# Mixture-of-experts stage with tiles of 128 slots in place of 256

## The reference

```python
def _L0_ffn_ref(x, gate_w, expert_bias, w_up, w_down):
    B, S, H, E, K, I = (4, 512, 256, 8, 2, 1024)
    logits = jnp.einsum('bsh,eh->bse', x, gate_w) + expert_bias
    weights = jax.nn.softmax(logits, axis=-1)
    top_w, top_i = jax.lax.top_k(weights, K)
    top_w = top_w / (jnp.sum(top_w, axis=-1, keepdims=True) + GATE_EPS)
    sparse_w = jnp.sum(jax.nn.one_hot(top_i, E, dtype=weights.dtype) * top_w[..., None], axis=-2)
    out = jnp.zeros_like(x)
    for e in range(E):
        h = jax.nn.gelu(jnp.einsum('bsh,ih->bsi', x, w_up[e]), approximate=False)
        y = jnp.einsum('bsi,hi->bsh', h, w_down[e])
        out = out + sparse_w[..., e:e + 1] * y
    mu = jnp.mean(out, axis=-1, keepdims=True)
    var = jnp.mean(jnp.square(out - mu), axis=-1, keepdims=True)
    out = (out - mu) * jax.lax.rsqrt(var + LN_EPS)
    return out + x
x = x + _L0_xattn_ref(_layernorm(x, axis=-1), ctx_1024, ctx_1024, L0_xattn_Wq, ...)
x = x + _L0_ffn_ref(_layernorm(x, axis=-1), L0_ffn_gate_w, ...)
```

## Time and profile before

| what | value |
|---|---|
| median of 3 runs | 841.6 us (840.79 to 843.38) |
| profiled execution, span | 841.2 us |
| TensorE matmuls busy | 738.7 us (88%) |
| VectorE / ScalarE / GpSimd busy | 561.5 / 363.6 / 443.2 us |
| mean granted TensorE clock | 0.932 of full |

### The profile page before, as it was taken

The page is one execution under the profiler, slowest core; times in us unless marked ns, Lnnn a source line. Parts: engine busy times, 40 slices in busy tenths (PEclk is TensorE's granted clock), DMA queues, the critical chain, the costliest instruction groups (busy, mean ns, idle before and its releaser), DMA issues.

```text
span 841.2 us, 20449 instructions
## 1 busy us (share of the span) xinstructions
PE 738.7 (88%) x6144; PEld 665.2 (79%) x6145; DVE 561.5 (67%) x1215; ACT 363.6 (43%) x657; POOL 443.2 (53%) x584
## 2 busy tenths in 40 slices
PE   4999999999999934599999999999999999999300
PEld 4899999999999832288989999999999999898200
DVE  4899898998989758565555555555555555554195
ACT  2777777777777711122222222222222222222185
POOL 3677777777777623534444444444444444432287
PEclk9999999999999965589999999999999999999755
DMA  4233333233232110011111111111111111110494
GB/s 154 94 103 107 114 98 108 99 106 112 96 115 91 51 39 0 25 39 52 52 51 50 50 50 44 44 50 50 45 49 44 50 50 50 50 37 26 144 312 169
DMA packets 39874, 64.52 MB, mean 77 GB/s; under 512 B 5408, under 2 KB 30240, under 8 KB 39840
## 3 DMA queue, kind: packets, MB, share of 16 engines
q1 hardware_dynamic: 31632, 42.37, 15.7%
q0 software_dynamic: 7488, 20.46, 7.6%
q10 hardware_dynamic: 720, 1.26, 0.4%
HBM read 45.46 MB, written 18.61 MB: 76 GB/s over the span
## 4 chain that ended last, share of the span: by engine, by line
PE 87%; DVE 4%; issue 3%; POOL 2%; DMA 1%; ACT 1%; SPq 0%; DVEq 0%; POOLq 0%; ACTq 0%
PE ps_a L527 25%; PE ps_b L541 24%; PE ps_a L387 7%; PE ps_b L430 7%; PE ps_c L409 3%; PE ps_c L414 3%; PE ps_b L397 3%; PE ps_a L465 3%; PE ps_a L452 2%; PE ps_c L495 2%; PE ps_c L511 2%; PE ps_a L476 1%; PE ps_c L377 1%; PE ps_a L440 1%; PE ps_c L422 1%
## 5 line engine op out<-in xcount | busy, mean ns | idle before, releaser
L527 PE MATMUL ps_a<-area,w_hi 128*128 128x256 f16 x1248 | 208.8, 274 | 1.7 <-DVE area L792 1.7
L541 PE MATMUL ps_b<-w_hi,area 128*128 x1248 | 206.4, 273 | 0.0
L1052 POOL DMA_INDIRECT y_rows<-area x78 | 78.0, 1001 | 209.2 <-ACT area L937 197.3
L527 PE MATMUL ps_a<-area,w_lo 128*128 128x256 f16 x624 | 171.1, 274 | 0.0
L541 PE MATMUL ps_b<-w_lo,area 128*128 x624 | 170.1, 273 | 0.0
L932 ACT ACTIVATE area<-ps_a 128x512 f32<-128x512 f32 x156 | 93.2, 598 | 143.1 <-PE ps_a L527 141.7
L527 PEld LDWEIGHTS ps_a<-area,w_hi 128*128 x1248 | 122.8, 98 | 16.4 <-issue 2.1
L541 PEld LDWEIGHTS ps_b<-w_hi,area 128*128 128x128 f16 x1248 | 122.1, 98 | 14.1
L790 DVE TENSOR_SCALAR area<-ps_c 128x512 f16<-128x512 f32 x39 | 27.0, 692 | 151.7 <-PE ps_c L511 151.7
L802 DVE SCALAR_TENSOR_TENSOR area<-area 128x512 f16<-128x512 f32 x156 | 108.3, 694 | 5.4
L1042 POOL DMA_INDIRECT area<-xn_rows,area x78 | 77.7, 996 | 46.9 <-issue 35.9
(11 more groups left out here) (130 smaller groups left out, 1263.8 us busy)
## 6 DMA issues: line engine op xcount, KB each, us to landing
area<-weights SPq DMA_DIRECT2D x32, 512.0 KB, 3.3
w_hi<-y_rows SPq DMA_DIRECT2D x32, 256.0 KB, 4.6
resid<-x_in SPq DMA_DIRECT2D x32, 128.0 KB, 2.1
area<-ctx_t SPq DMA_DIRECT2D x32, 128.0 KB, 2.1
xn_rows<-area SPq DMA_DIRECT2D x32, 128.0 KB, 1.7
out<-w_lo SPq DMA_DIRECT2D x16, 256.0 KB, 2.7
area<-xn_rows,area POOLq DMA_INDIRECT x78
y_rows<-area POOLq DMA_INDIRECT x78
```

The source lines that it names most:

```text
L527: mm = pe.matmul(ps_h[:, q, (ic % 2) * SLOTS:(ic % 2 + 1) * SLOTS], w[:, bass.ds(first + (hc * I + ic * P), P)], r[b][:, hc, :], start=(n ...
L541: mm = pe.matmul(ps_y[:, b, v * D:(v + 1) * D], g[b][:, ic, v * P:(v + 1) * P], w[:, bass.ds(first + (EXPERT_COLS + ic * D), D)], start=(n ...
L1052: pool.indirect_dma_start(y_rows[:, :], bass.IndirectOffsetOnAxis(ap=didx[b][:, v:v + 1], axis=0), y_s[b][:, v * D:(v + 1) * D], None).the ...
```

## The change

SUBS goes from 2 to 1, so a tile has 128 slots and there are 71 tiles. A gather, a scatter, and one of down's two passes over the 24 products fall away from each tile; up keeps its 48 matmuls and 48 weight loads a tile, with 128 moving columns. Four chunks now fill a PSUM bank, so a tile's h takes two banks, GQ is 2, and two tiles of h lie in PSUM and two in g_s. Waits on g_r and gl_r go back two tiles in place of one. The loop covers tiles 4 to 68.

```diff
-SUBS = 2
+SUBS = 1
...
-        GQ = 4
-        g_s = [carve(512) for _ in range(GQ)]
+        GQ = 2
+        g_s = [[carve(512) for _ in range(GQ)] for _ in range(2)]
...
-        MOE_FIRST, MOE_LAST = 4, 36
+        MOE_FIRST, MOE_LAST = 4, 68
...
-                    q = ic // 2
-                    if ic % 2 == 0:
-                        since(pe, g_r, GQ * (k - 1) + q + 1)
+                    q, i = ic // (IC // GQ), ic % (IC // GQ)
+                    if i == 0:
+                        since(pe, g_r, GQ * (k - 2) + q + 1)
                     n = 0
                     for hc in range(HC):
                         for w, r in ((w_hi, xt_hi), (w_hi, xt_lo), (w_lo, xt_hi)):
-                            mm = pe.matmul(ps_h[:, q, (ic % 2) * SLOTS:(ic % 2 + 1) * SLOTS],
+                            mm = pe.matmul(ps_h[:, GQ * b + q, i * SLOTS:(i + 1) * SLOTS],
                                            w[:, bass.ds(first + (hc * I + ic * P), P)], r[b][:, hc, :],
                                            start=(n == 0), stop=(n == 3 * HC - 1))
                             n += 1
-                    if ic % 2:
+                    if i == IC // GQ - 1:
                         mm.then_inc(h_ps, 1)
...
-                    src = ps_x[:, b, :].rearrange("p (c n) -> p c n", c=HC)
+                    src = ps_x[:, b, 0:HC * SLOTS].rearrange("p (c n) -> p c n", c=HC)
...
-                        src = g_s[q].rearrange("p (c n) -> p c n", n=SLOTS)
+                        src = g_s[b][q].rearrange("p (c n) -> p c n", n=SLOTS)
...
-                        since(act, gl_r, GQ * (k - 1) + 1 + q)
-                        act.activation(g_s[q], ps_h[:, q, :], ACT.Gelu, scale=1.0 / (X_SCALE * W_SCALE)).then_inc(g_r, 1)
+                        since(act, gl_r, GQ * (k - 2) + 1 + q)
+                        act.activation(g_s[b][q], ps_h[:, GQ * b + q, :], ACT.Gelu, scale=1.0 / (X_SCALE * W_SCALE)).then_inc(g_r, 1)
...
-                    act.activation(y_s[b], ps_y[:, b, :], ACT.Copy, scale=1.0 / (G_SCALE * W_SCALE)).then_inc(y_r, 1)
+                    act.activation(y_s[b], ps_y[:, b, 0:SUBS * D], ACT.Copy, scale=1.0 / (G_SCALE * W_SCALE)).then_inc(y_r, 1)
```

## The result

The changed kernel takes 979.67 us (median of 4 runs, 978.93 to 979.96) where the kernel before takes 842.01 (median of 4, the three known ahead of the prediction and one more): a ratio of 1.163, 95% interval 1.162 to 1.165. The prediction said 974, range 940 to 1030, slower with 0.94. The profiled execution of the changed kernel took 978.93 us and has a span of 977.1: 1.8 us of a launch lie outside the span, where the text ahead of the prediction has nothing. The prediction's 974 is added up from a span, so it is to be held against 977.1.

A forecast was written before the change was run, and what follows sets the result against it. TensorE's array bounds the expert stage before; after the change its sequencer does, 7.94 us a tile against 5.5 of array. Span 841.2 + 136.8 (stage) - 3.8 (small terms) = 974 us, range 940 to 1030 (its own 950 to 1005).

The forecast's parts named there:

- The bound: Expert stage after the change: TensorE's sequencer needs 7.94 us a tile against 5.5 of array, stage +136.8 us.
- The turn: Expert loop on the sequencer, two tiles: first tile 8.26 us, second 7.61; a loop turn of 15.9 us.
- the groups of three matmuls: Up and down: three matmuls with their register instructions take 0.24 us of sequencer, 16 groups in up, 8 in down.
- The reads: Expert number read ahead of up and down: 0.75 to 0.9 us each, 1.5 with the loop's turn, no longer hidden.
- The small terms: Outside the tile loop: first gather -1.3, last scatter -1.3, routing products -1.3, larger expert table +0.1; together -3.8 us.
- The array as the bound: Rival, expert stage: sequencer keeps ahead, a tile costs 5.5 us, kernel gains, 802 us; chance 0.05.
- Reads that hide: Rival, expert stage: only up's 80 ns pace counts, reads and loop turn hide behind queued matmuls, 885 us; chance 0.05.
- Loads that do not hide: Rival, up: 128-column matmuls stay at 109 ns, 8.1 us of array a tile, 999 us; chance 0.05.
- The falling clock: Rival, expert stage: TensorE idle about a third, clock falls; a third of tiles at low clock, 1040 us; chance 0.07.
- the second set of h banks: PSUM banks and g_s in the expert stage: second set removes waits that before does not show; costed at nothing.
- the gathers two tiles ahead: Expert stage: a tile's gather is issued two tiles ahead, 16 us, where landing took 2.8; costed at nothing.
- the other engines: Expert stage, per tile: VectorE 3.0 us, ScalarE 1.5, GpSimd about 3.5, each under 7.94, so off the path.

The follow-up runs named there:

- the test of the reads alone: Changed kernel without the two reads of slot_expert a tile, weights' place worked out from the tile's number, register instructions kept in the loop: 875.39 us, ratio 1.040.

## Why the prediction was right

**The bound.** It moved where the prediction put it: from the array to TensorE's sequencer. Constant addresses take 178 us away at 128 slots and none at 256, and the loop's turn is the sum of the sequencer's own steps.

**The terms.** The turn was forecast at 15.87 us and is 16.18. Up and down together take 12.0 us of the sequencer in a turn where 11.72 were forecast, so the groups of three matmuls take 0.25 us and not 0.24. The reads were within 0.1 us each. The loop makes 32 turns (64 tiles, 4 to 67). From its entry at 386.8, the second line below, to its last branch at 904.9 they take 518.1 us, 10.3 more than the forecast has for them. The rest of the stage, seven tiles, first matmuls and drain, takes 55.5 us, 4.5 less than the 60.0 left for it; these tiles have no turn, and no further cause of the 4.5 is shown. The stage runs from the transposes at 350.28 to the last matmul's end at 923.62 + 0.27, 573.6 us, where 567.8 was forecast:

```profile
350.28 0.66 PE L511 MATMUL ps_c<-cst,area 128*128 128x128 f32 x2 [5.60 <-DMA area<-xn_rows,area]
...
L290 PEldq MOVE  x1: 29/29/29, 386.8 to 386.8; - x1
...
352.08 0.39 PE L527 MATMUL ps_a<-area,w_hi 128*128 128x128 f16 x2 [1.14 <-DVE area L792]
...
923.62 0.27 PE L541 MATMUL ps_b<-w_lo,area 128*128 x1
```

**The small terms** were forecast at -3.8 and came to -6.7: the stage begins 3.7 us earlier than in the earlier trace rows, and from the last matmul to the end it is 53.2 us in place of 56.2. In the first, the routing matmuls take 16.90 us in place of 18.25 and the first gather leads to the first transposes in 3.0 us (347.25 to 350.28) in place of 4.5; each is close to its forecast of -1.3. Another 0.9 us lie ahead of them, and 0.7 of these arise between 300 and 305 us, at the end of attention, which the change leaves alone. There the same matmuls ran at the low clock in the trace before (first line, granted clock 0.50 from 301.0 to 301.8) and still at 1.00 in the trace after (second line):

```profile
301.01 0.70 PE ps_a L440 x2
...
300.94 0.45 PE ps_a L440 x2
```

That is chance between two executions. In the second part, one scatter less is 1.5 us, and the other 1.5 lie in the combine, which the change leaves alone too. In sum 142.6 - 6.7 = +135.9 us on spans of 841.2 and 977.1.

**What was luck.** The mechanism and the terms were right, but that the sum came within 3 us of the span is partly luck. The loop was forecast 10 us too short; the tiles outside it gave 4.5 us back and the small terms 2.9, of which some 2 have nothing to do with the change.

**The rivals.** The array as the bound (802 us) is what constant addresses give, 801.99: its price was right and its condition false. That the two agree to the microsecond is luck: its terms were rounded more coarsely than that. Reads that hide (885) fell with the test of the reads alone, 0.7 us each on the path. Loads that do not hide (999) fell with 56 ns a pair. The falling clock did not come, at 1.00 over the stage. It came in the run with half of up's columns, where it cost 0.9 us a turn.

**Costed at nothing:** the second set of h banks (3 to 4 us), the gathers two tiles ahead, and the other engines; no wait on them is in the trace beyond the one group read above.

## What to carry to other kernels

Before cutting matmuls smaller, count what the sequencer does between them: register instructions for addresses, reads of a register from memory, branches, waits. At 256 slots all of it was hidden behind the engine's queue, so the trace of before had to be asked for it separately, in stretches where the sequencer's steps are shorter than the engine's. If its sum per tile comes near the array's, a smaller tile can make the kernel slower even though the array has less to do. Constant addresses gave the time back here; addresses used twice kept it hidden in the kernel before.

## What the runs showed of the hardware

- A 128-column f16 matmul with its own weight load takes 56 ns at clock 1.00 when no register instruction stands between (2.68 us for 48), and 85 ns with two register instructions for three matmuls. With 64 columns it takes 30 ns where the sequencer has run ahead (0.71 us for 24), and 84 ns where it has not.
- Reading one number from SBUF into a register with its bounds check takes 0.7 us of TensorE's sequencer: leaving out four of them took 2.8 us off a loop turn.
- The clock can fall in a stage in which TensorE stands still for 1.1 us at the longest: with up matmuls of 64 columns at 84 ns it was 0.50 in about every second down, with 128 columns at 85 ns it stayed at 1.00. Taking work out of the array made the kernel 27 us slower.
- Leaving one expert's loop for the next one's code cost 3.5 to 3.6 us at clock 1.00 and 4.2 to 4.4 where the clock fell after it, with two reads of bounds, one of the expert and three branches in it, and with down's addresses from a register in the first tile; how much of that is fetching code is open.
